# Local attention: the band mask added by VectorE, and the two rotary half products joined in one reversed operation

## The reference, cut to what matters

```python
DEPTH, HEADS, DIM_HEAD, WINDOW, QK_SCALE = 6, 16, 64, 32, 8.0
qkv = shift_tokens(x) @ Wqkv                    # x: [4, 512, 128]
q, k, v = split(qkv, 3)                         # 16 heads of 64
q, k = l2norm(q) * q_scale, l2norm(k) * k_scale
q = q * cos * scale + rotate_half(q) * sin * scale
k = k * cos * inv + rotate_half(k) * sin * inv  # rotate_half: cat(-x2, x1)
# windows of 32 queries look at their own and the previous 32 keys
mask = (it < jb) | (it > jb + w) | (jb == -1)
sim = einsum('bhwie,bhwje->bhwij', q, look(k)) * QK_SCALE
attn = softmax(where(mask, -max, sim))
out = einsum('bhwij,bhwje->bhwie', attn, look(v)) @ Wo
```

## Time and profile before

| | |
|---|---|
| median of 3 runs | 5445.45 us (5443.71 to 5460.72) |
| profiled execution, its own time | 5470.13 us |
| its span | 5468.3 us |
| mean granted TensorE clock of the span | 0.901 of full speed |
| busy share of the span | PE 84%, PE weight loads 51%, DVE 56%, ACT 52%, POOL 36% |

### The profile page before, as it was taken

One profiled execution on the slowest core, in us unless ns is written; L12 is line 12 of the kernel. 1 busy time (PEld: TensorE's weight loads), 2 busy tenths in 40 slices (PEclk: granted clock), 3 DMA queues, 4 the chain that ended last, 5 costly groups with the idle time before them and its releaser, 6 DMA issues. The chain is left out here.

```text
span 5468.3 us, 100163 instructions
## 1 busy us (share of the span) xinstructions
PE 4578.9 (84%) x36268; PEld 2790.6 (51%) x36268; DVE 3078.7 (56%) x5928; ACT 2838.8 (52%) x8700; POOL 1977.2 (36%) x2122
## 2 busy tenths in 40 slices
PE   2998869897998988988979889865557988887999
PEld 1665446575564664645646646534445664223344
DVE  6453155355664755746647557539994555662433
ACT  2453224454774765747747657457772442452522
POOL 0231000033984957939849579203331320000000
PEclk6899969899998999999999999976778998896889
DMA  0000000000111111111111111100000000000000
GB/s 33 23 1 4 2 22 9 17 2 7 45 46 38 46 46 38 41 39 46 46 38 46 46 34 45 35 20 1 1 1 11 1 4 5 10 5 32 6 0 8
DMA packets 34484, 123.02 MB, mean 22 GB/s; under 512 B 8484, under 2 KB 9512, under 8 KB 32296
## 3 DMA queue, kind: packets, MB, share of 16 engines
q1 hardware_dynamic: 33960, 116.23, 7.9%
HBM read 37.24 MB, written 1.05 MB: 7 GB/s over the span
## 5 line engine op out<-in xcount | busy, mean ns | idle before, releaser
L640 POOL MEMSET norm_eps<- 128x1 f32 x16 | 1.6, 98 | 1680.8 <-POOLq L116 1621.8
L2095 POOL TENSOR_TENSOR local_other<-local_raw,local_sin 128x256 f32<-128x256 f32 x768 | 557.3, 726 | 60.2
L1956 PE MATMUL ps<-arena,local_xs 128*128 128x512 f32 x768 | 438.9, 656 | 111.0 <-DVE local_raw L2136 61.5
L2092 POOL TENSOR_TENSOR local_rot<-local_raw,local_cos 128x512 f32<-128x512 f32 x384 | 488.2, 1271 | 68.4 <-DVE local_raw L2136 68.3
L2098 POOL TENSOR_TENSOR local_rot<-local_rot,local_other 128x512 f32<-128x512 f32 x384 | 486.6, 1267 | 30.1
L2069 ACT ACTIVATE ps<-ps,local_negmax 128x96 f32<-128x96 f32 x1536 | 474.2, 309 | 40.5 <-DVE local_negmax L2130 40.4
L2136 DVE SCALAR_TENSOR_TENSOR local_raw<-local_inverse,ps 128x512 f32<-128x512 f32 x384 | 264.0, 688 | 275.5 <-ACT local_inverse L2063 275.5
L2126 DVE TENSOR_REDUCE local_norm<-local_squares 128x8 f32<-128x512 f32 x384 | 263.2, 685 | 133.3 <-ACT local_squares L2038 133.3
L2038 ACT ACTIVATE local_squares<-ps 128x512 f32<-128x512 f32 x384 | 229.8, 598 | 158.1 <-PE ps L1956 157.8
L2069 ACT ACTIVATION_READ_ACCUMULATOR ps<-ps,local_negmax 128x1 f32 x1536 | 309.8, 202 | 0.0
L2001 PE MATMUL ps<-const,local_probs 128*96 128x128 f32 x1536 | 235.3, 275 | 77.8 <-DVE local_probs L2154 77.8
(11 more groups left out here) (527 smaller groups left out, 10969.1 us busy)
## 6 DMA issues: line engine op xcount, KB each, us to landing
local_V_span<-local_V SPq DMA_DIRECT2D x96, 384.0 KB, 4.0
local_V_span<-local_V SPq DMA_DIRECT2D x96, 256.0 KB, 3.6
arena<-in_L1f_a SPq DMA_DIRECT2D x7, 2176.0 KB, 8.5
local_V_span<-local_V SPq DMA_DIRECT2D x72, 128.0 KB, 2.3
arena<-in_L3f SPq DMA_DIRECT2D x1, 3460.0 KB, 10.9
arena<-in_L1f_f SPq DMA_DIRECT2D x6, 537.5 KB, 4.0
arena<-in_L0f SPq DMA_DIRECT2D x1, 2824.5 KB, 10.0
arena<-in_L0x SPq DMA_DIRECT2D x1, 2049.5 KB, 9.1
```

Source lines behind the costliest of these rows:

```text
L1956: nc.tensor.matmul(bank("qk", n)[:, :], tokens_of(tile), w("Wqkv", QKV[i] * 512, (QKV[i] + 1) * 512), start=True, stop=True)\
L2092: link(nc.gpsimd.tensor_tensor(rot, raw, m.cos[:, t, a * DH:(a + 1) * DH].unsqueeze(1) .broadcast_to([P, 8, DH]), ALU.mult))
L2095: link(nc.gpsimd.tensor_tensor(other[:, :, lo:lo + HALF], raw[:, :, HALF - lo:DH - lo], m.sin[:, t, a * DH + lo:a * DH + lo + HALF].unsque ...
```

## The change: what it does

VectorE adds the mask to the scores, in place in PSUM, right before the maximum, with a wait between the two; the mask comes straight from the constants, broadcast over the four groups. TensorE no longer writes the mask, and each small product of queries and keys starts fresh instead of accumulating. The buffers `unit` and `bands`, and the three copies that filled them once, are gone. On GpSimd the two half products become one instruction whose input runs over the two halves in reversed order.

```diff
-        self.unit = tmp("unit", [P, P], BF16)
-        self.bands = tmp("bands", [P, 2, 4, SPAN], BF16)
...
+    def halves(a):
+        return a.rearrange("p (h j f) -> p h j f", j=2, f=HALF)
...
-                    edge = int(tile % QT == 0 and half_span == 0)
-                    for i in range(2):
-                        nc.tensor.matmul(SC[(s + i) % 3][:, 0:UNITS * SPAN], m.unit[:, :],
-                                         m.bands[:, edge, :, :].rearrange("p u k -> p (u k)"), start=True, stop=False)
...
-                                                      m.K[rows, c, first:first + SPAN], start=False,
-                                                      stop=(u == UNITS - 1))
+                                                      m.K[rows, c, first:first + SPAN], start=True, stop=True)
...
-                for lo in (0, HALF):
-                    link(nc.gpsimd.tensor_tensor(other[:, :, lo:lo + HALF], raw[:, :, HALF - lo:DH - lo],
-                                                 m.sin[:, t, a * DH + lo:a * DH + lo + HALF].unsqueeze(1)
-                                                 .broadcast_to([P, 8, HALF]), ALU.mult))
+                link(nc.gpsimd.tensor_tensor(halves(m.other[:, :]), halves(m.raw[:, n % 4, :])[:, :, ::-1, :],
+                                             m.sin[:, t, a * DH:(a + 1) * DH].rearrange("p (j f) -> p j f", f=HALF)
+                                             .unsqueeze(1).broadcast_to([P, 8, 2, HALF]), ALU.mult))
...
                     dve.wait_ge(scores_ready, s // 2 + 1)
+                    tile, half_span, _ = place(s)
+                    band = core.c("band_first" if tile % QT == 0 and half_span == 0 else "band")
+                    link(nc.vector.tensor_tensor(sc, sc, band.unsqueeze(1).broadcast_to([P, UNITS, SPAN]), ALU.add))
                     nc.vector.tensor_reduce(m.negmax[:, s % 2, :], sc, AX_X, ALU.max, negate=True)\
                       .then_inc(max_ready, 1)
...
-                nc.vector.tensor_copy(bufs.unit[:, :], core.ident).then_inc(copied, 1)
-                for i, name in enumerate(("band", "band_first")):
-                    nc.vector.tensor_copy(bufs.bands[:, i, :, :], core.c(name).unsqueeze(1).broadcast_to([P, 4, SPAN]))\
-                      .then_inc(copied, 1)
```

## The result

The median went from 5451.43 us (7 runs, 5443.71 to 5468.10) to 5503.77 us (7 runs, 5488.23 to 5523.03). The ratio is 1.009, with a 95% interval of 1.0066 to 1.0115: the change makes the kernel 0.9% slower. The forecast was 5443 us, no measurable change, with a range up to 5475; the result lies outside. Medians are compared, since single executions scatter: of twenty of the kernel before, three took 5506 to 5511 us, at a mean granted clock of 0.891 to 0.895 where the others had 0.898 to 0.906.

The account below looks back on a forecast made before the run. No engine is full; a chain of waits across TensorE, ScalarE and VectorE bounds the tile. Six layers of -0.6 (tiles), -1.6 (start), +1.9 (end) give -2 us: 5443 on the median, range 5413 to 5475.

Parts of the forecast that it names:

- The addition's price: VectorE's mask addition in PSUM: 0.56 us plus 0.04, so 0.60 from its start to the maximum's; bounds 0.55 and 0.73.
- Masks off TensorE: Settled tile: two masks leave TensorE's chain at 0.42 us each, 0.84 a tile; with nothing else, 16.95 us.
- The chain of a settled tile: Settled tiles: a chain through two VectorE additions replaces the masks' chain; 17.79 to 17.75 us, at most -0.6 a layer.
- The waits forecast: Settled tile: TensorE waits about 1.2 us for probabilities; ScalarE's 1.14 us wait for transposes is replaced by waits for the maximum.
- The start of a layer: First pieces and first tile of a layer: GpSimd's piece falls from 4.17 to 3.92 us, together -1.6 us a layer.
- The end of a layer, +1.9: Last seven steps of a layer: each VectorE addition lies on the chain, adding 1.9 us a layer.
- The clock: Rival at a layer's end: TensorE waits longer, its clock falls; about 3 us a layer, 18 us, 5461; chance 0.07.
- in the settled part TensorE stays busy: Argument against a larger clock loss: TensorE stays busy 205 of 230 us, 89%, in the settled part without masks.
- the dearer addition: Rival: PSUM access makes VectorE's addition cost more than 0.60 us, deciding from 0.68; at 0.73, 5469 us; chance 0.18.

Follow-up runs that it names:

- both masks: Changed kernel with TensorE's two mask products kept as well and overwritten by the scores: 5506.45 us, ratio 1.0084 to the kernel before.
- no mask at all: Changed kernel with VectorE's addition left out too, so the mask is missing from the computation: 5377.68 us, ratio 0.9865 to the kernel before.
- the mask by turns: Changed kernel, but TensorE makes the mask in odd steps and the last seven, VectorE adds it in the other even steps: 5420.08 us, ratio 0.9936.
- the rotary product alone: Kernel before with only GpSimd's two half products joined into one; masks stay on TensorE: 5447.20 us, ratio 0.9968.
- the mask alone: Kernel before with only the mask moved to VectorE; GpSimd's two half products stay separate: 5491.82 us, ratio 1.007.

## Why the prediction failed, by its own steps

The prediction's sum was -0.3 us a layer (-0.6 - 1.6 + 1.9); measured are +6.9. Of the 7.2 between them 4.3 are the clock, 1.4 the tiles, 1.3 the start of a layer, and 0.2 the end at a held clock.

- **The addition's price: right.** The addition took 556 ns where 0.56 was taken from L2154, with the maximum 0.59 behind it where 0.60 was.
- **Masks off TensorE: mis-sized.** The prediction took the distance from the mask's start to the scores' start, 0.42 us each. On the chain a mask is worth 0.33: one adds 0.33 a tile (both masks), two give 0.65 (no mask at all).
- **The chain of a settled tile: right in mechanism.** 17.79 to 17.75 was forecast from the starts of products in one tile; by maxima, the tiles grew by 0.04 instead of shrinking by up to 0.04, and by the product of the rows above from 17.77 to 17.81. The two kernels that move that chain, both masks and the mask by turns, came within 0.10 and 0.08 of their sums. Over a layer the term is +0.8 where up to -0.6 stood, of which 0.39 is the tile of 18.09.
- **The waits forecast.** TensorE waits 1.06 us for the probabilities (1.2 forecast), and 0.71 instead of 0.42 for the scaling ahead of a product, 0.29 more where 0.31 was said. ScalarE's wait of 1.14 for the transposes is not replaced but shortened, to 0.81, and the waits for the maximum stand beside it. The first layer's first maximum comes 26.43 us after its start instead of 27.96, 1.5 sooner where 1.3 was said; that was luck. In the third to sixth layers it comes 0.6 later (27.32 to 27.34, and 26.70 before), and in the first layer the maximum of step 4 is already 0.7 later than before.
- **The start of a layer: mis-sized.** The step "together -1.6 a layer" took GpSimd's saving and forgot the additions in the same steps. The joined product alone gives -2.1 there, more than forecast; with the additions it is -0.34 to the maximum of step 4 and -0.4 with the second tile. GpSimd keeps its saving: in the third layer its sixteenth piece starts 65.70 us after the layer's start, 65.73 with the rotary product alone and 69.58 before. The softmax steps hand most of it back: at equal clock (idle products with and without the mask moved, third layer) the maximum of step 0 comes 0.6 us later, that of step 4 1.3 and that of step 8 2.0.
- **The end of a layer, +1.9: right only while the clock holds.** With it held in both kernels the last seven steps and the end cost 0.66 + 1.80 - 0.32 = 2.1 us. As run, they cost 5.8, of which 3.7 is the next step.
- **The clock: this is the step that failed.** The sum has the products at a layer's end at their old lengths, so it puts the clock at nothing; the prediction had the mechanism as a rival with a price of 3 us a layer, and gave it 0.07. Measured are 3.7 us a layer in the attention part (5.3 less the 1.6 that holding the clock gives the kernel before), and 0.6 more in the feed-forward behind it, where the clock of the start went from 0.69 to 0.60. At six layers that is 26 us of some 41. What spoke against it, "in the settled part TensorE stays busy", was right (1.00 in the row above), but it argued about the wrong stretch: the rival's own place was the end, and there two facts in the rows spoke for it. The clock was already 0.87 in the first layer, so some products there ran at the lower level; and the additions and the missing masks both thin TensorE's work in just these steps. The range was also too narrow by the prediction's own prices: the dearer addition (5469) and the clock (18) together are 5487, not 5475. The 5503.77 measured lies above even that, without a dearer addition: the clock cost 4.3 a layer and not 3, and the start and the tiles took 2.6 more than their terms.

The Trainium skill (TensorE: Matmul & The Clock Gate, A second HAM failure mode: psum-queue depth-cycling) says that frequent short idle moments between groups of products can send the clock back and forth, and cost throughput. Here the runs agree at the end of a layer: waits of 1.94 and 2.34 us between groups, a clock of 0.68, and 5.3 us back with idle products in three steps.

What stays open: why the one tile from step 20 to 24 takes 18.09 (it does so in the changed kernel, with the mask alone and with the idle products, and in no other kernel here). In it VectorE's scaling of step 20 starts at 2201.09 in the third layer, 0.45 us after ScalarE's exponential L2059 that it reads has ended (2200.43 and 0.21 long), where it is 0.10 a tile earlier; what holds it, the trace does not name. Open is also how the fall of the clock divides between the missing masks and the added waits. With no mask at all it dropped to 0.75 in two layers, and with both masks it stood at 0.81 to 0.87, so each seems to have a part; but the clock differs from layer to layer within one run, and each kernel has one trace. The layers also began 7.5 us sooner after the change (1338.9 and 1346.5); the kernel before with idle products, which keeps the three setup copies, begins them at 1339.0 as well, so that is a difference between executions and not the copies.

## What to carry to other kernels

Work moved off a busy engine is worth its time only on the chain that remains: here masks worth 0.65 us a tile bought nothing, because a chain through the other engine, as long to within 0.04 us, took its place, while moving only the half that had slack gave 0.3 a tile. A place where TensorE already waits and its clock is under 1.00 is to be priced apart from the settled loop, and twice: once for the waits, once for what the products that the chain waits for cost at the lower level. Idle products in the waits, on kernels with and without the change, separate the two prices and may be worth keeping.

## What the runs showed of the hardware

- VectorE adding in place in PSUM costs what writing to SBUF does: 556 ns for 128x384 with one operand broadcast from SBUF, against 557. The next instruction, waiting for it, starts 0.03 to 0.04 us after its end.
- GpSimd reads two halves in reversed order at the usual rate: 1274 ns for 128x512, against 1.27 us for a product in plain order; one instruction saves 0.25 us over two of half the size.
- The kernel gained time from added work on TensorE. Three idle products of 1.13 us each a layer took the granted clock of the last 27 us from 0.68 to 1.00, from a mix of the two levels of 1.2 and 2.4 GHz to the higher one alone; the projection went from 3.78 to 2.05 us, and the attention part became 5.3 us shorter. The same products in the kernel before, with 0.94 there, gave 1.6 us.
